# Down weight operands prepared at other places in the order of steps, and the two staging tiles of a block product added onto the result by two transfers in a row

## What is computed

```
def reference(x, qkv, o_proj, gamma, beta, w_gate, w_up, w_down):
    xn = layernorm(x)
    # attention: x_norm = layernorm(xn) * gamma + beta; q, k, v = x_norm @ qkv
    # scores = q k^T * scale, causal; out = softmax(scores) @ v @ o_proj + xn
    # feed forward on xn:
    h = silu(xn @ w_gate) * (xn @ w_up)          # 2048 x 2048
    h_sparse = h, of each 4 neighbours the 2 largest by magnitude kept
    ffn = h_sparse @ w_down                       # 2048 x 512
    return x + attention(xn) + ffn
```

## Time and profile before

| | us |
|---|---|
| median of three runs | 797.4 |
| lowest, highest of them | 796.82, 801.81 |
| the profiled execution | 800.95 |
| its span in the profile | 799.2 |
| PE busy in the span | 785.4 (98%) |
| DVE busy | 630.1 (79%) |
| ACT busy | 365.4 (46%) |
| POOL busy | 62.9 (8%) |

### The profile page before, as it was taken

How to read it: one execution, slowest core, us unless ns; L and a number is a source line. 1 busy time by engine, 2 the same in 40 slices (tenths; PEclk the granted TensorE clock), 3 DMA queues, 4 the chain that set the end, 5 groups by cost and what they waited for, 6 DMA issues and landing times.

```text
span 799.2 us, 9954 instructions
## 1 busy us (share of the span) xinstructions
PE 785.4 (98%) x3734; PEld 658.5 (82%) x3734; DVE 630.1 (79%) x998; ACT 365.4 (46%) x600; POOL 62.9 (8%) x70
## 2 busy tenths in 40 slices
PE   9999999999997999999999999999999999999998
PEld 7888888878886887788887888888898898898887
DVE  6979788688753698779989788699778669669786
ACT  5423351235222364554547537355554464465541
POOL 2011110010010000010100010100101100100100
PEclk9999999999999999999999999999999999999999
DMA  9441705511244438486747869599757767665602
GB/s 321 180 160 59 233 0 208 181 71 54 107 155 160 155 131 309 144 321 251 249 104 258 321 134 358 137 422 325 227 221 234 214 248 230 181 231 112 157 2 106
DMA packets 40240, 153.26 MB, mean 192 GB/s; under 512 B 3648, under 2 KB 4224, under 8 KB 36992
## 3 DMA queue, kind: packets, MB, share of 16 engines
q1 hardware_dynamic: 28080, 122.66, 40.3%
q0 software_dynamic: 10816, 27.79, 15.4%
q10 hardware_dynamic: 1296, 2.16, 0.8%
HBM read 85.99 MB, written 66.62 MB: 191 GB/s over the span
## 4 chain that ended last, share of the span: by engine, by line
PE 65%; DMA 2%; ACT 1%; DVE 1%; issue 1%; SPq 0%; DVEq 0%; ACTq 0%
PE bank L1094 12%; PE bank L1095 12%; PE bank L1096 12%; PE bank L1177 4%; PE bank L1179 4%; PE bank L1178 4%; PE bank L1210 3%; PE bank L1212 3%; PE bank L1211 3%; PE bank L832 2%; PE bank L834 2%; PE bank L833 2%; DMA X_raw<-block_sums 1%; DMA wsum<-w_units 1%; DMA result<-rows 1%
## 5 line engine op out<-in xcount | busy, mean ns | idle before, releaser
L1094 PE MATMUL bank<-X_hi,wset 128*128 128x512 f32 x448 | 175.6, 392 | 4.0 <-ACT bank L1409 3.0
L1096 PE MATMUL bank<-X_hi,wset 128*128 128x512 f32 x448 | 175.1, 391 | 0.0
L1095 PE MATMUL bank<-X_lo,wset 128*128 128x512 f32 x448 | 175.0, 391 | 0.0
L1094 PEld LDWEIGHTS bank<-X_hi,wset 128*128 128x128 f32 x448 | 84.5, 189 | 23.3 <-ACT bank L1409 4.2
L1096 PEld LDWEIGHTS bank<-X_hi,wset 128*128 128x128 f32 x448 | 84.5, 189 | 17.8
L1095 PEld LDWEIGHTS bank<-X_lo,wset 128*128 128x128 f32 x448 | 84.5, 189 | 17.0
L825 POOL DMA_DIRECT2D result<-staged x26 | 31.5, 1213 | 333.0 <-ACT staged L1482 116.9
L832 PE MATMUL bank<-zg,xT 128*128 128x512 f32 (+2 forms) x132 | 50.6, 383 | 4.2 <-ACT wide_raw L1388 4.2
L834 PE MATMUL bank<-zg,xT 128*128 128x512 f32 (+2 forms) x132 | 49.9, 378 | 0.0
L833 PE MATMUL bank<-zg,xT 128*128 128x512 f32 (+2 forms) x132 | 49.9, 378 | 0.0
L1177 PE MATMUL bank<-dw,hs_hi 128*128 128x512 f32 x128 | 49.9, 389 | 0.0
(11 more groups left out here) (294 smaller groups left out, 1746.5 us busy)
## 6 DMA issues: line engine op xcount, KB each, us to landing
w_operands<-wset SPq DMA_DIRECT2D x8, 3584.0 KB, 13.5
wset<-w_operands SPq DMA_DIRECT2D x8, 3584.0 KB, 12.1
result<-staged POOLq DMA_DIRECT2D x26, 512.0 KB, 5.5
down_operands<-prep POOLq DMA_DIRECT2D x6, 1792.0 KB, 8.5
wsum<-w_units SPq DMA_DIRECT2D x28, 256.0 KB, 4.0
dwop<-down_operands SPq DMA_DIRECT2D x3, 2048.0 KB, 11.4
dwop<-down_operands SPq DMA_DIRECT2D x3, 1536.0 KB, 11.9
xw<-L_attn_x SPq DMA_DIRECT2D x4, 1024.0 KB, 9.9
```

The costliest lines, as they stand in the source:

```text
L1094: pe.matmul(dst[:], u[:, 0, :], x_hi, start=(first and kt == 0), stop=False, skip_group_check=True)
L1095: pe.matmul(dst[:], u[:, 0, :], x_lo, start=False, stop=False, skip_group_check=True)
L1096: last = pe.matmul(dst[:], u[:, 1, :], x_hi, start=False, stop=(kt == 1), skip_group_check=True)
```

## The change

It moves steps of the preparation of the down weight operands, and it takes out the DVE addition of the staging tiles.

- Part 0: sums and high casts go from unit 3 to 5 of chunk 2 to behind its maxima; the low halves go into the softmax of chunk 2. Its load also waits until the rows of chunk 1 are done. Part 1: sums and casts go from within the softmax of chunk 2 to its end. Part 2: sums and casts go behind the first two row tiles of unit 3, which themselves stay.
- The row sums of chunk 3 (`sum_turn`) are read by DVE before, not after, the last low half of X (`X_lo`).
- Part 4: the sums go behind the last results of stage 0, the casts into stage 1 behind `up_seed`, the low halves ahead of the first hidden tile of stage 1. Its load waits for the load of T4. Part 5: its two casts go between the copies of the down product of stage 3.
- Block products: POOL adds `staged[1]` and then `staged[2]` onto the rows; the second of these waits for the first (`first_added`). ACT's copy of P7 waits for the second transfer of the block before (`pair_added[1]`), that of P6 for the first (`first_added`).

```
-              *prep_sum[0], *u[4:6], *prep_hi_steps[0], xn[2][1], xn_store[2], u[6], ...
-              xh_pre[3][3], xh[3][2], *u[10:], ..., xh[3][3], *prep_lo[0], prep_store[0], prep_load[1], *z_round[3], *z[3][0:2]]
-    steps += softmax(2, {-1: [z[3][2]], ...},
-                     {3: prep_sum[1], 4: [*prep_hi_steps[1], xn[3][0]], 5: [xn[3][1], xn_store[3]]})
-    steps += [*prep_lo[1], prep_store[1], prep_load[2], ("sum_turn", 2, 0), ...
+              *u[4:6], xn[2][1], xn_store[2], u[6], ...
+              xh_pre[3][3], xh[3][2], *u[10:], ..., xh[3][3], *prep_sum[0], *prep_hi_steps[0], *z_round[3], *z[3][0:2]]
+    steps += softmax(2, {-1: [prep_lo[0][0], z[3][2]], ...},
+                     {1: [prep_lo[0][1], prep_store[0], prep_load[1]], 4: [xn[3][0]], 5: [xn[3][1], xn_store[3]]})
+    steps += [*prep_sum[1], *prep_hi_steps[1], *prep_lo[1], prep_store[1], prep_load[2], ("sum_turn", 2, 0), ...
...
-    steps += [*u[0:2], *prep_sum[2], u[2], *prep_hi_steps[2], u[3], *rows_of[2][2], ("rows_load", OLD + 8, 0), *rows_of[2][3], ("rows_load", OLD + 9, 0),
-              *prep_lo[2], prep_store[2], prep_load[3], *u[4:6], ("w_sum", 0, 0), u[6], *w_hi_steps[0:2], ...
+    steps += [*u[0:4], *rows_of[2][2], ("rows_load", OLD + 8, 0), *rows_of[2][3], ("rows_load", OLD + 9, 0), *prep_sum[2], *u[4:6], *prep_hi_steps[2],
+              *prep_lo[2], prep_store[2], prep_load[3], ("w_sum", 0, 0), u[6], *w_hi_steps[0:2], ...
...
-    steps += [("T4_load", 0, 0), *X_lo_steps[2:4], *X_hi_steps[5:], *X_lo_steps[4:], ("sum_turn", 3, 0), ...
+    steps += [("T4_load", 0, 0), *X_lo_steps[2:4], *X_hi_steps[5:], *X_lo_steps[4:6], ("sum_turn", 3, 0), X_lo_steps[6], ...
@@ POOL, load_prep @@
+                    pool.wait_ge(rows_ready, OLD + TC)        # p == 0
+                if p == PREP_FIRST:
+                    pool.wait_ge(T_loaded[T4], 16)
@@ POOL, the additions onto the result, b == 1 of a block product @@
-                        pool.wait_ge(staged_summed, block_no(i) + 1)
+                        nc.gpsimd.dma_start(out_tiles[tile:tile + 2]..., staged[1][:], accum_op=ALU.add).then_inc(first_added, 16)
+                        pool.wait_ge(first_added, 16 * (block_no(i) + 1))
-                    nc.gpsimd.dma_start(out_tiles[tile:tile + 2]..., staged[b][:], accum_op=ALU.add
+                    nc.gpsimd.dma_start(out_tiles[tile:tile + 2]..., staged[2 if b and i in BLOCKED else b][:], accum_op=ALU.add
                                         ).then_inc(pair_added[b], 16)
@@ ACT, keep_part @@
                 elif k == D_P7:
-                    act.wait_ge(staged_summed, block_no(i))
+                    if block_no(i):
+                        act.wait_ge(pair_added[1], 16 * i)
                 elif k == D_P6:
-                    act.wait_ge(pair_added[1], 16 * i)
+                    if block_no(i):
+                        act.wait_ge(first_added, 16 * block_no(i))
+                    else:
+                        act.wait_ge(pair_added[1], 16 * i)
@@ ACT, stages @@
+                if n == 1:                                     # behind up_seed(n)
+                    prep_operands_hi(PREP_FIRST, 0)
+                    prep_operands_hi(PREP_FIRST, 1)
-                if n == 0:                                     # ahead of last_silu(n)
-                    prep_operands_hi(PREP_FIRST, 0)
-                    prep_operands_hi(PREP_FIRST, 1)
                     for t in range(TC):
                         keep_down(i, t)
-                    if n == 3:
-                        prep_operands_hi(PREP_LATE, 0)
-                        prep_operands_hi(PREP_LATE, 1)
+                        if n == 3 and t < 2:
+                            prep_operands_hi(PREP_LATE, t)
@@ DVE, stages @@
+                if n == 1:                                     # ahead of first_hidden(n)
+                    prep_operands_lo(PREP_FIRST, 0)
+                    prep_operands_lo(PREP_FIRST, 1)
                 if n == 0:                                     # behind last_block(n)
-                    prep_operands_lo(PREP_FIRST, 0)
-                    prep_operands_lo(PREP_FIRST, 1)
+                    prep_sums(PREP_FIRST, 0)                   # before: ahead of last_block(n)
+                    prep_sums(PREP_FIRST, 1)
-                    sum_staged(i)                              # i in BLOCKED
```

More of the change, by code:

```diff
@@ L140, in attention_ffn @@
     steps += [*u[0:2], *rows_of[1][2], *rows_of[1][3], ("rows_load", OLD + 4, 0), ("rows_load", OLD + 5, 0), *u[2:4], xn[2][0],
-              *prep_sum[0], *u[4:6], *prep_hi_steps[0], xn[2][1], xn_store[2], u[6], xh_pre[3][0], u[7], xh_pre[3][1], xh[3][0], u[8], xh_pre[3][2], xh[3][1], u[9],
-              xh_pre[3][3], xh[3][2], *u[10:], ("max_fold", 2, 0), ("max_all", 2, 0), xh[3][3], *prep_lo[0], prep_store[0], prep_load[1], *z_round[3], *z[3][0:2]]
-    steps += softmax(2, {-1: [z[3][2]], 0: [z[3][3]], 1: v[2][0:2], 2: v[2][2:4]},
-                     {3: prep_sum[1], 4: [*prep_hi_steps[1], xn[3][0]], 5: [xn[3][1], xn_store[3]]})
-    steps += [*prep_lo[1], prep_store[1], prep_load[2], ("sum_turn", 2, 0), *rows_of[2][0], ("rows_load", OLD + 6, 0), *rows_of[2][1],
+              *u[4:6], xn[2][1], xn_store[2], u[6], xh_pre[3][0], u[7], xh_pre[3][1], xh[3][0], u[8], xh_pre[3][2], xh[3][1], u[9],
+              xh_pre[3][3], xh[3][2], *u[10:], ("max_fold", 2, 0), ("max_all", 2, 0), xh[3][3], *prep_sum[0], *prep_hi_steps[0], *z_round[3], *z[3][0:2]]
+    steps += softmax(2, {-1: [prep_lo[0][0], z[3][2]], 0: [z[3][3]], 1: v[2][0:2], 2: v[2][2:4]},
+                     {1: [prep_lo[0][1], prep_store[0], prep_load[1]], 4: [xn[3][0]], 5: [xn[3][1], xn_store[3]]})
+    steps += [*prep_sum[1], *prep_hi_steps[1], *prep_lo[1], prep_store[1], prep_load[2], ("sum_turn", 2, 0), *rows_of[2][0], ("rows_load", OLD + 6, 0), *rows_of[2][1],
               ("rows_load", OLD + 7, 0)]
@@ L151, in attention_ffn @@
     w_hi_steps, w_lo_steps = fills("w_hi", 0), fills("w_lo", 0)
-    steps += [*u[0:2], *prep_sum[2], u[2], *prep_hi_steps[2], u[3], *rows_of[2][2], ("rows_load", OLD + 8, 0), *rows_of[2][3], ("rows_load", OLD + 9, 0),
-              *prep_lo[2], prep_store[2], prep_load[3], *u[4:6], ("w_sum", 0, 0), u[6], *w_hi_steps[0:2], *u[7:9], *w_lo_steps[0:2], *u[9:], ("max_fold", 3, 0),
+    steps += [*u[0:4], *rows_of[2][2], ("rows_load", OLD + 8, 0), *rows_of[2][3], ("rows_load", OLD + 9, 0), *prep_sum[2], *u[4:6], *prep_hi_steps[2],
+              *prep_lo[2], prep_store[2], prep_load[3], ("w_sum", 0, 0), u[6], *w_hi_steps[0:2], *u[7:9], *w_lo_steps[0:2], *u[9:], ("max_fold", 3, 0),
               ("max_all", 3, 0), ("X_load", 0, 0), v[3][0], v_keep[0], *v[3][1:4]]
@@ L158, in attention_ffn @@
                       6: [X_lo_steps[0], v_keep[3], X_hi_steps[1], X_hi_steps[2]], 7: [X_lo_steps[1], X_hi_steps[3], X_hi_steps[4]]})
-    steps += [("T4_load", 0, 0), *X_lo_steps[2:4], *X_hi_steps[5:], *X_lo_steps[4:], ("sum_turn", 3, 0), *rows_of[3][0], *rows_of[3][1], *rows_of[3][2], *rows_of[3][3]]
+    steps += [("T4_load", 0, 0), *X_lo_steps[2:4], *X_hi_steps[5:], *X_lo_steps[4:6], ("sum_turn", 3, 0), X_lo_steps[6], *rows_of[3][0], *rows_of[3][1], *rows_of[3][2], *rows_of[3][3]]
     def key_tiles(i):
@@ L371, in attention_ffn @@
         op_step, op_hi_ready, op_ready = sem("op_step"), sem("op_hi_ready"), sem("op_ready")
-        part_full, part_kept, staged_summed = sem("part_full"), sem("part_kept"), sem("staged_summed")
+        part_full, part_kept, first_added = sem("part_full"), sem("part_kept"), sem("first_added")
         full = [sem("gate_full"), sem("up_full")]
@@ L821, in _ @@
                     else:
-                        pool.wait_ge(staged_summed, block_no(i) + 1)
+                        nc.gpsimd.dma_start(out_tiles[tile:tile + 2].rearrange("t p d -> p t d"), staged[1][:], accum_op=ALU.add).then_inc(first_added, 16)
+                        pool.wait_ge(first_added, 16 * (block_no(i) + 1))
                     if (i, b) == (2, 0):
                         store_prep(PREP_LATE)
-                    nc.gpsimd.dma_start(out_tiles[tile:tile + 2].rearrange("t p d -> p t d"), staged[b][:], accum_op=ALU.add
+                    nc.gpsimd.dma_start(out_tiles[tile:tile + 2].rearrange("t p d -> p t d"), staged[2 if b and i in BLOCKED else b][:], accum_op=ALU.add
                                         ).then_inc(pair_added[b], 16)
@@ L2026, in operand_lo @@
                 nc.vector.tensor_tensor(op_lo[k][:], op_source(i, k), op_hi[k][:].bitcast(F32), ALU.subtract).then_inc(op_ready, 1)
-            def sum_staged(i):
-                dve.wait_ge(part_kept, NOP * block_no(i) + D_P4)
-                nc.vector.tensor_tensor(staged[1][:], staged[1][:], staged[2][:], ALU.add).then_inc(staged_summed, 1)
             def last_block(n):
```

3 lines of the change are left out of this document (removed).

## The result

The changed kernel took 809.8 us (median of four runs, 809.0 to 811.5) against 798.7 us for the kernel before on the same chip (four runs, 796.8 to 801.8): a ratio of 1.0138, 95% interval 1.0098 to 1.0178. It is slower by 11.1 us where 805.5 us had been forecast. The profiled execution took 811.5 us, its span is 809.7 us.

What follows compares the result with a forecast made beforehand. PE was taken to bound the kernel. A cost of 20.0 us less gains of 13.7 made 6.3 us more: 807.3 us from the profiled execution's time, 803.7 otherwise; the middle, 805.5, was forecast, own range 799 to 813.

Steps and rivals of the forecast that it cites:

- The bound: Whole kernel: PE-bound, other engines' work pays only where PE waits; five waits with their slow clock worth 15.1 us.
- The moves: Preparation steps in chunks 2 and 3 and stages 0 to 4: gain 13.7 us, bounds 9 and 15.1.
- In chunk 3 I left 1.0 us: Chunk 3, PE's wait for ACT's score copy: 1.0 of 4.2 us left; gain 4.8 us, bounds 1.8 and 5.8.
- In chunk 2 I left 0.4 us: Chunk 2, PE's wait for ACT's score copy: 0.4 of 1.9 us left; gain 3.2 us, bounds nothing and 3.6.
- The waits for the row sums and at stages 0 to 1 and 3 to 4: Chunk 3's row sums and the copies that seed stages: waits go whole, gains 1.0, 3.5 and 1.2 us.
- The DVE additions, forecast nothing: Block products: taking out six DVE additions of 1.2 us gains nothing, as PE doesn't wait there.
- Products 1, 3 and 5: Block products 1, 3 and 5: three transfer slots end 4.4 us before the next copy of P7, no cost.
- Products 2 and 4: Block products 2 and 4: third slot meets the `wset` load, PE waits; cost 20.0 us, bounds 1.7 and 29.
- The lower price for a transfer from POOL: Third slot by the Trainium skill: 3.2 us for 512 KB, so no PE wait; the prediction set it against its trace.
- The level: Starting time for the sum: ending at 807.3 (profiled execution's own time) or 803.7 us; middle taken, 805.5.
- "No wait": Rival, block products: third slot gets through beside `wset`, no PE wait; 785.5 us, or 787 with 1.7 left; chance 0.13.
- "Also in other products": Rival: third slot starves in other products too, or chunk 2 and 3 gains stay out; 813 us and more; chance 0.05.

Runs made afterwards that it cites:

- the moves alone: Kernel before with only the moved preparation steps, keeping the DVE addition and two transfers per block product: 785.8 us, ratio 0.9833.
- the halves above: Two runs on the kernel before: only the moves of parts 0 to 2 and the row sums, 789.6 us; only those of parts 4 and 5, 793.2 us.
- the third transfer only: Kernel before with the DVE addition replaced by a third POOL transfer and no moved steps: 823.1 us, ratio 1.0301.
- the moves in chunks 2 and 3: Kernel before with only the moves of parts 0 to 2 of the down weights and the row sums: 789.6 us, ratio 0.9896.
- the load was held: Changed kernel with SP holding the `wset` load behind block products 2 and 4 until the third addition has landed: 790.8 us, ratio 0.9907.
- the kernel with room for two transfers: Changed kernel with 1536 instead of 1024 bytes a partition for the descriptors of POOL's transfers: 787.5 us, ratio 0.9862.

## Why the forecast held in sign and was short in size

**The bound.** PE waits and the clock behind them decided, and nothing else: the span of the moves alone (783.7) without its 1.3 us of waits, plus the waits and the slow clock of any other kernel's profile, gives that kernel's span within 0.9 us.

**The moves, forecast 13.7 us.** Measured 13.4 by the medians (11.5 to 15.3 by the interval), 15.5 by the spans (799.2 to 783.7). By halves: chunks 9.0 forecast, 9.0 measured; stages 4.7 forecast, 5.4 measured, with the row sums' 1.0 us in both (see the halves above), where the forecast had it in the chunks alone. Inside that, two sizes were off. In chunk 3 I left 1.0 us; nothing was left here or in the moves alone. DVE's first weight sum came 8.0 us earlier, which its timeline shows (answers to the earlier trace rows):

```profile
240.66 0.42 DVE L1631 TENSOR_TENSOR wsum<-wsum 128x256 f32<-128x256 f32 x1 [3.88 <-DMA wsum<-w_units]
```

Of these 8.0 us, 2.1 are chunk 3 as a whole starting earlier (ACT's first score copy at 219.18 instead of 221.26); the other 5.9 stand against the 3.2 of the forecast and the wait of 4.2.

In chunk 2 I left 0.4 us; the changed kernel shows 1.0, the moves alone 0.3. With the order unchanged the wait is 1.9 us in one profile, 1.3 in another and absent in a third. So 3.2 us was forecast from an execution that had it in full, and against the median it is too much by an amount that no run here tells. The clock behind a wait is no fixed price either: the wait of 1.8 us ahead of stage 1 has 1.7 us of slow clock behind it in the profile before, and none in those of the third transfer only and of the moves in chunks 2 and 3. That the sum came out near 13.4 is in part luck: too little was taken in chunk 3, and too much where the profile before was slower than the median. The waits for the row sums and at stages 0 to 1 and 3 to 4 went whole, as forecast.

**The DVE additions, forecast nothing.** Right, by the run without them (785.8 us with and without).

**Products 1, 3 and 5, forecast no cost.** Right: PE has no wait there.

**Products 2 and 4, forecast 20.0 us.** The mechanism was right in place, number and cause: two waits, the third slot issued within a microsecond of `wset`, starved by it. The size was short: 24 us by the medians of the kernels with and without it (809.8 - 785.8, and 23.8 on the kernel before), 25.2 by the trace (9.6 + 2.5 + 10.2 + 2.9). The mis-sized terms are these. The wait was put at 8.3 us and is 9.6 and 10.2: the slot took 13.4 and 13.9 instead of 13.0, and the second slot with its gap took 6.2 and 6.1 instead of the 5.5 of a slot alone, so the third went out that much later. The clock behind was put at 1.7 us, from waits of 2 to 4 us, and is 2.5 and 2.9 behind waits of 10. The premise that an accumulating transfer isn't issued before the one ahead has landed holds for the descriptor space of these two kernels only: with 1536 bytes the second went out after 0.7 us, and neither wait came. The lower bound, 5.5 us as alone, was nearly met when the load was held (5.6 to 5.9).

**The lower price for a transfer from POOL.** The Trainium skill's page "DMA: Bandwidth & Descriptors", section "Anatomy of one DMA — SWDGE (gpsimd) path", gives by its figures an estimate of 3.2 us for 512 KB. By that estimate the third slot of product 2 would have landed at 606.5 (603.34 + 3.2), and neither wait would be there. No addition in any run here took under 5.2 us, so no run agrees.

**The level.** I took the middle between 807.3 (own time) and 803.7 (median). With gains and costs as measured the additive sum on the median is 798.7 - 13.4 + 23.8 = 809.1, and 809.8 was measured. The middle stands for a kernel before of 799.2 us, 0.5 above the median measured beside the change, so the level was hardly an error by itself; the 4.3 us between 805.5 and 809.8 are almost all the cost, which was short by 4.

**The rivals.** "No wait" is what the kernel with room for two transfers shows, at 787.5 (forecast for this rival 785.5 to 787): there the third slot goes out 2.2 us ahead of the load with nothing else beside it, which the changed kernel doesn't reach. "Also in other products" didn't happen.

## What to carry to other kernels

When a producer waits for a buffer that a queued transfer must empty, count the slots of that queue one after the other, and look which large load is issued beside the last of them: here 512 KB took 5.5 us alone and 13.4 beside 3.5 MB, and 1.2 us of DVE work that cost nothing was given for it. Take the two halves of a change apart before judging it: this one is 13.4 us of gain and 24 us of loss, and the better kernel is the half. A transfer whose engine idles before it with "issue" as the reason may want nothing but room for its descriptors; half as much again brought the whole change from 809.8 to 787.5 us.

## What the runs showed of the chip that I had not expected

An addition from POOL sends its first packet 1.8 us after its issue when nothing runs beside it, and 3.8 to 4.9 us after when a large load of SP's is in flight, whether that load had begun 0.7 us before (603.34 to 607.8 in the changed kernel) or 5.4 us before (584.64 to 589.1). The kernel before has it too (599.11 to 603.6). Rows of 4 KB instead of 28 KB left this delay as it was. Why is open; a run that separates it wasn't made.

A load can be kept out as well. Where the addition's packets came first (from 604.2 on in the kernel with room), `wset`, issued at 604.62, had its first packet only 2.5 us later, at 607.1; in the changed kernel, where no addition was sending, it had them 1.0 us after its issue (602.62 to 603.6).

Waits of 1.0 us in chunk 2 and of 1.4 us in chunk 3 left the clock at 1.00, a wait of 1.8 us did in two profiles out of three; behind waits of 2.7 (with the load held), 9.6 and 10.2 us (in the changed kernel) it was at 0.50 for about 3.4, 5.0 and 5.8 us of PE's work. Two waits of one length don't cost the same: behind that of 4.3 us in the kernel with the third transfer only, 2.9 us were lost to the clock, behind that of 4.2 in the kernel before 1.6.
